# Retention scores: masked queries moved 512 columns wide over four row quarters, in place of masked keys loaded 128 wide over two

## The reference

```python
qh, kh, vh = (heads(q), heads(k), heads(v))          # [B, 16, T, 8]
gammas = decay_gammas(H)
dmask = jnp.where(causal[None], gammas[:, None, None] ** exponent[None], 0.0)
sim = jnp.einsum('bhnd,bhmd->bhnm', qh, kh) * scale
sim = sim * dmask[None]
yh = jnp.einsum('bhnm,bhmd->bhnd', sim, vh)
y = yh.transpose(0, 2, 1, 3).reshape(B, T, D)
y = y @ ow.T + ob
x = residual + y
```

## Time and profile before

| | before |
|---|---|
| median of 3 runs | 2216.85 us |
| lowest, highest | 2211.02, 2219.46 us |
| span of the profiled execution | 2256.3 us |
| TensorE busy | 1912.8 us (85%) |
| VectorE busy | 1357.7 us (60%) |
| ScalarE busy | 1044.8 us (46%) |
| GpSimd busy | 319.3 us (14%) |
| mean granted clock of TensorE | 0.821 of full |
| retention stage | about 900 to 1037 us of the span |

### The profile page before, as it was taken

How to read it: one execution, slowest core, us unless ns; L and a number is a source line. 1 busy time by engine, 2 the same in 40 slices (tenths; PEclk the granted TensorE clock), 3 DMA queues, 4 the chain that set the end, 5 groups by cost and what they waited for, 6 DMA issues and landing times.

```text
span 2256.3 us, 35340 instructions
## 1 busy us (share of the span) xinstructions
PE 1912.8 (85%) x12022; PEld 1293.6 (57%) x12022; DVE 1357.7 (60%) x4960; ACT 1044.8 (46%) x2490; POOL 319.3 (14%) x455
## 2 busy tenths in 40 slices
PE   6887777787778799999999888888899954999888
PEld 4464566666666566886555776555454542973333
DVE  3777888888888644676333485542121431569886
ACT  2433555665566423333444223454344313437667
POOL 0001000000000000330000002003126023406642
PEclk9999666667676568898999657998999967988989
DMA  2001100000000000000001100003013200635662
GB/s 111 1 13 36 32 22 22 19 19 25 19 19 19 34 1 1 2 3 2 0 1 75 40 1 1 1 15 97 13 12 50 89 14 30 113 69 91 98 103 40
DMA packets 93282, 76.09 MB, mean 34 GB/s; under 512 B 22320, under 2 KB 85168, under 8 KB 92336
## 3 DMA queue, kind: packets, MB, share of 16 engines
q1 hardware_dynamic: 85424, 65.31, 12.8%
q0 software_dynamic: 7680, 8.53, 2.0%
HBM read 48.86 MB, written 23.51 MB: 32 GB/s over the span
## 4 chain that ended last, share of the span: by engine, by line
PE 56%; DVE 23%; ACT 6%; DMA 4%; issue 4%; SPq 3%; another core or an unknown queue 1%; POOL 1%; DVEq 0%; PEld 0%; PEldq 0%; ACTq 0%; POOLq 0%
PE ps L204 52%; DVE sm L225 8%; ACT big L213 3%; DVE mw L225 3%; DMA d_pt<-big 3%; DVE big L217 2%; PE ps L208 2%; PE ps L2465 2%; SPq L2552 1%; DVE big L231 1%; DVE tmp L221 1%; ACT sm L213 1%; SPq L866 1%; DVE big L225 1%
## 5 line engine op out<-in xcount | busy, mean ns | idle before, releaser
L213 ACT ACTIVATE tmp<-ps,bi 128x512 f32<-128x512 f32 (+1 forms) x226 | 153.9, 684 | 200.8 <-PE ps L204 189.3
L204 PE MATMUL ps<-big,mw 128*128 128x512 f32 (+3 forms) x476 | 236.3, 593 | 11.6 <-DVEq L252 5.6
L213 ACT ACTIVATE sm<-sm 128x1 f32<-128x1 f32 x512 | 174.4, 341 | 106.6 <-DVE sm L225 96.0
L204 PE MATMUL ps<-ke,big 32*128 32x128 f32 (+2 forms) x1632 | 154.0, 296 | 62.3 <-ACT big L212 61.8
L204 PE MATMUL ps<-big,co 128*128 128x256 f32 (+1 forms) x360 | 180.5, 636 | 27.9 <-DMA bi<-bia 12.2
L213 ACT ACTIVATE big<-ps,co 128x512 f32<-128x512 f32 (+1 forms) x296 | 174.5, 648 | 61.3 <-PE ps L204 58.2
L204 PEld LDWEIGHTS ps<-ke,big 32*128 32x128 f32 (+2 forms) x1632 | 132.3, 195 | 87.4 <-ACT big L212 72.0
L231 DVE TENSOR_REDUCE big<-ps 128x2 f32<-128x512 f32 x256 | 161.2, 675 | 21.0 <-PE ps L204 20.7
L204 PE MATMUL ps<-ke 48*128 48x256 bf16 (+4 forms) x638 | 127.5, 315 | 34.7 <-DVE big L217 16.7
L204 PE MATMUL ps<-big,tmp 128*32 128x256 f32 (+2 forms) x1180 | 137.5, 424 | 22.9 <-DVE tmp L221 17.6
L217 POOL TENSOR_TENSOR big<-big,co 128x512 f32<-128x512 f32 x32 | 40.1, 1274 | 765.6 <-ACT big L212 765.6
(11 more groups left out here) (254 smaller groups left out, 3834.5 us busy)
## 6 DMA issues: line engine op xcount, KB each, us to landing
mw<-d_tab SPq DMA_DIRECT2D x32, 328.0 KB, 3.4
mw<-m SPq DMA_DIRECT2D x2, 4096.0 KB, 12.7
d_pt<-big SPq DMA_DIRECT2D x32, 192.0 KB
ke<-d_pt SPq DMA_DIRECT2D x72, 64.0 KB
big<-d_pt SPq DMA_DIRECT2D x72, 64.0 KB
mw<-d_pt SPq DMA_DIRECT2D x48, 64.0 KB
d_xs<-big SPq DMA_DIRECT2D x1, 2560.0 KB, 15.3
big<-d_xs SPq DMA_DIRECT2D x5, 512.0 KB, 6.4
```

The costliest lines, as they stand in the source:

```text
L204: return e.matmul(out, lhsT, rhs, start=start, stop=stop)
L213: return e.activation(out, in_, f, bias=K("zero")[0:out.shape[0], :] if bias is None else bias, scale=scale, **kw)
```

## The change

Three things change together.

The mask moves from the keys to the queries. ScalarE makes masked copies of the queries (`QM`, four instructions a block as before). The stationary operand is now a quarter of the plain keys (32 x 128), and the moving operand is the same quarter of all four masked queries, 32 x 512. One matmul gives the four heads of a quarter, and a half needs four matmuls, which are issued one after another as one burst and wait together.

The score banks rotate. A half takes two pairs of banks out of three pairs (banks 0 and 1, 2 and 3, 4 and 5), by the count `(2 * hh + p) % 3`. Its four matmuls wait for the first mask of the half before. Values, transposed keys and state move to bank 6, and the output of the block and its projection share bank 7. For that `ret_y_pe` now waits in first halves for the residual addition of the block before (`re_xa`) where it waited for a copy, and `ret_out_pe` and `ret_add_dve` move later: block n-2 is projected and added during block n, after the first scores of block n, and the addition stands ahead of the masks of block n on VectorE.

A mask covers two banks: four instructions of 128 x 1024 a block in place of eight of 128 x 512. On ScalarE the copy of the output (`ret_yc_act`) moves behind the copies of values and keys.

```diff
-        def ret_scores_pe(e, s):
-
-            n, h, p = s // 4, s // 2 % 2, s % 2
+        def pair(hh, p):
+            k = 2 * ((2 * hh + p) % 3)
+            return slice(k, k + 2)
+
+        def ret_scores_pe(e, hh):
+
+            n, h = hh // 2, hh % 2
             i, c0 = n % 2, n * S + 128 * h
-            if s % 4 == 0:
-                e.wait_ge(*re_km(4 * n + 4))
-            if s > 1:
-                e.wait_ge(*re_sm(2 * (s - 2) + 2))
-            for r in range(4):
-                for g in (2 * p, 2 * p + 1):
-                    q = mm(e, PS[:, g, 128 * r:128 * r + 128], KM[i][r32(g), r, 128 * h:128 * h + 128], QF[r32(g), c0:c0 + 128])
-                    if r == 3:
-                        q.then_inc(re_s.sem, 1)
+            if h == 0:
+                e.wait_ge(*re_qm(4 * n + 4))
+            if hh:
+                e.wait_ge(*re_sm(2 * hh - 1))
+            for g in range(4):
+                mm(e, PS[:, pair(hh, g // 2), :][:, g % 2, :], KF[r32(g), c0:c0 + 128], QM[i][r32(g), :, 128 * h:128 * h + 128]).then_inc(re_s.sem, 1)
...
             if h:
                 e.wait_ge(*re_sbd(n + 1))
-            elif n > 1:
-                e.wait_ge(*re_yc(n - 1))
-            e.wait_ge(*re_sm(4 * hh + 4))
+            elif n:
+                e.wait_ge(*re_xa(n))
+            e.wait_ge(*re_sm(2 * hh + 2))
...
-            for s in range(4 * NB + 2):
-                n, k = s // 4, s % 4
+            for hh in range(2 * NB + 2):
+                n, h = hh // 2, hh % 2
                 if n < NB:
-                    ret_scores_pe(e, s)
-                if s > 2 and k % 2:
-                    ret_y_pe(e, (s - 3) // 2)
-                if k == 1 and n + 1 < NB:
+                    ret_scores_pe(e, hh)
+                if h == 0 and n > 1:
+                    ret_out_pe(e, n - 2)
+                if h == 0 and n + 1 < NB:
                     ret_vk_pe(e, n + 1)
-                if k == 2 and 0 < n < NB:
-                    ret_out_pe(e, n - 1)
-                if k == 3 and n + 1 < NB:
+                if hh > 1:
+                    ret_y_pe(e, hh - 2)
+                if h == 1 and n + 1 < NB:
                     ret_kv_pe(e, n + 1)
...
-                act(e, KM[i][:, r, :], KF[:, c0:c0 + S], ACT.Identity, scale=K("rm", r, r + 1)).then_inc(re_km.sem, 1)
+                act(e, QM[i][:, r, :], QF[:, c0:c0 + S], ACT.Identity, scale=K("rm", r, r + 1)).then_inc(re_qm.sem, 1)
...
-            for s in range(4 * NB):
-                n, k, hh = s // 4, s % 4, s // 2
-                for g in (2 * (s % 2), 2 * (s % 2) + 1):
+            for hh in range(2 * NB):
+                n, h = hh // 2, hh % 2
+                if h == 0 and n > 1:
+                    ret_add_dve(e, n - 2)
+                for p in range(2):
                     if hh > 2:
                         e.wait_ge(*re_y(hh - 2))
-                    e.wait_ge(*re_s(2 * s + g % 2 + 1))
-                    tt(e, S1[hh % 3][:, g, :].rearrange("p (r n) -> p r n", r=4), PS[:, g, :].rearrange("p (r n) -> p r n", r=4),
-                       K("tri").rearrange("p (r n) -> p r n", r=1).broadcast_to((128, 4, 128)), MU).then_inc(re_sm.sem, 1)
-                if k == 3 and n:
-                    ret_add_dve(e, n - 1)
-                if k == 3 and n + 1 < NB:
+                    e.wait_ge(*re_s(4 * hh + 2 * p + 2))
+                    tt(e, S1[hh % 3][:, 2 * p:2 * p + 2, :].rearrange("p g (r n) -> p (g r) n", n=128),
+                       PS[:, pair(hh, p), :].rearrange("p g (r n) -> p (g r) n", n=128),
+                       K("tri").rearrange("p (r n) -> p r n", r=1).broadcast_to((128, 8, 128)), MU).then_inc(re_sm.sem, 1)
+                if h == 1 and n + 1 < NB:
                     ret_sbd_dve(e, n + 1)
```

## The result

The changed kernel takes 2176.07 us (median of four runs, 2175.51 to 2180.28) and the kernel before, measured beside it, 2216.22 us. The ratio is 0.9838 with a 95% interval of 0.9815 to 0.9861: 40 us faster, where 24.5 were forecast.

| comparison | before | changed | gain | ratio, 95% interval |
|---|---|---|---|---|
| first | 2216.22 | 2176.07 | 40.2 | 0.9838, 0.9815 to 0.9861 |
| second | 2215.17 | 2184.84 | 30.3 | 0.9860, 0.9835 to 0.9884 |
| third | 2257.86 | 2228.89 | 29.0 | 0.9868, 0.9828 to 0.9907 |
| fourth | 2217.82 | 2188.13 | 29.7 | 0.9865, 0.9849 to 0.9880 |

The account below looks back on a forecast made before the run. TensorE was taken to bound the stage: 1.67 us a block times 14.3 is 23.9, plus half of 1.5 at half clock, together 24.5, so 2216.85 - 24.5 = 2192.3 us. The range of 8 in 10 was 2182 to 2207.

Parts of the forecast that it names:

- What bounds it: In the stage's even part TensorE sets the pace, one block of 7.87 us after another, while other engines wait.
- Four abreast: TensorE's score burst: all four row quarters run side by side, 1.06 us a burst, saving 1.72 us a block.
- Rival A: Score bursts: four quarters of 512 columns go only two abreast, period 7.9 us, time 2217; chance 0.09 with partly abreast bursts.
- The mask: VectorE's mask of 128 x 1024: 1.22 us by itself, 1.14 behind another, bounds 1.07 and 1.37.
- Rival B: VectorE and its waits take over: mask 1.37 gives period 6.5 and 2197 us, mask 1.6 gives 2207; chance 0.09.
- The walk: One block followed through TensorE and VectorE: addition waits for projection, second burst for the first mask; period 6.2 us.
- The even blocks: Stage at full clock: 14.3 blocks, each going from 7.87 to 6.2 us, 23.9 us in all.
- The start of the stage: 17.7 us at half clock: a block goes from 12.11 to 10.3 us, worth 1.5 us, half taken by the tail.
- rival C: Clock stays at 1.2 GHz as TensorE stands still for VectorE; 2251 us with all 14.3 blocks low; chance 0.06.
- the prediction's own sign: Forecast is wrong if the stage is not 20 to 28 us shorter, or it is and the whole is not.

Follow-up runs that it names:

- wide start: Kernel before, with only the first two of its 16 blocks scored by masked queries moved 512 wide: 2210.2 us against 2217.8, ratio 0.9971.
- two orders: Changed kernel with projection issued ahead of the first burst, or the next block's state matmul moved ahead of the projection: ratios to the kernel before 0.9865 and 0.9889.
- wide scores alone: Kernel before with masked queries and 512-column score matmuls only; its two quarters a step, banks, order and masks kept: ratio 0.9936 to the kernel before.

## Why the prediction was wrong

**What bounds it, right.** TensorE set the pace and its pieces were the right unit of account: every piece that was to stay stayed within 0.1 us.

**Four abreast, right.** 1.07 a burst against 1.06. Rival A is out, as eight records of 512 columns take 1.14 together. An estimate from the 3.07 of the Trainium skill (TensorE: Matmul & The Clock Gate, Measured speedup vs the span model) gives 1.32 with the change of shape. The trace does not bear that out for a stream of bursts; the timeline's 1.07 decides.

**The mask, right.** 1.217 against 1.22, over two banks of PSUM. Rival B is out. The Trainium skill (TensorEngine Tiling (Array Packing), PSUM Bottleneck) says that the copy out of PSUM may become the bottleneck once TensorE is four times faster; the prediction put that as a certainty. The trace comes near it without reaching it: VectorE is busy for 53.00 of 61.96 us and the second burst waits for its first mask, but TensorE sets the period.

**The walk, right.** Period 6.2, addition late by 0.7, second burst held by the mask. It is right for a slightly other reason in the sum: projection and values next to each other take 1.29 instead of 1.38, and the wait for the mask takes that back.

**The even blocks, right.** Thirteen intervals of 7.87 became 6.20, 21.7 us, and the two last ones went from 9.88 to 9.27 together: 22.3 us against 23.9 forecast.

**The start of the stage, wrong. This is the step that failed.** The prediction said: "In the 17.7 us at half clock a block takes 12.11 before and an estimated 10.3 after", worth 1.5 us, half of it spent again. (Its terms, 23.9 and 0.75, add to 24.65 where it wrote 24.5.) It took the length of the low clock from the earlier trace rows as given and priced only the work inside it. From the stage's start to its first addition it is 24.2 us before and 17.1 after: 7.1 us, not 0.8. The clock stands at half for 6.4 to 6.5 us instead of 20 (once 13). The wide start in an otherwise unchanged kernel is enough for it, holding two quarters back in four bursts undoes it, and with 128 columns at a time it is the same (6.4), so it is shown that issuing four quarters abreast at the stage's start brings it. Why the clock answers to that is not shown. The prediction had this cause in its hands and gave it the wrong sign: rival C argued that waits keep the clock down, and in its answer stands that TensorE "does more in a unit of time than before", but no gain was drawn from that.

The stage then gives 7.1 + 22.3 = 29.4 us, the measured 136.8 to 107.4, and the three repeats of the comparison 29.0 to 30.3. By the prediction's own sign (a stage 20 to 28 us shorter) the stage alone makes it wrong.

**The remaining 10 us of the first comparison stay open.** The time fell below the range by them, and no step of the prediction accounts for them. Its interval (0.9815 to 0.9861) overlaps those of all three repeats. The trace of the changed kernel that goes with its runs has the same stage of 107.4 us, and outside the stage it takes 2066.2 us, against 2074.4 and 2085.7 in the second and the fourth comparison; so the changed kernel won them outside the stage, where no instruction differs. No trace of the kernel before goes with these runs. Traces of one chip (that of the second comparison) lie between 2065.2 and 2082.1 there, whatever the kernel, so spread of four runs a side is likely and not shown. Without it the forecast of 24.5 would have been 5 us short.

## What to carry to other kernels

Where TensorE's work is cut in row quarters, count how many are in flight in a slot, not how busy the engine is: four quarters issued together, one matmul each into a bank of its own, cost what two did (1.07 against 1.06 us here). Where a stage starts at the low clock, the length of that stretch belongs to the sum as a term of its own: here it was anything from 6.3 to 37.0 us, by how the first burst was issued. Look at the first bursts of the stage and what holds them apart. And walk every order once with all the semaphores: two orders that looked 0.1 and 0.2 us a block better on TensorE alone came out 0.14 and 0.22 worse, for a copy and for a cut that were just in time before.

## What the runs showed of the hardware

- The granted clock did not go by TensorE's busy share. It stayed at 0.50 through stretches in which TensorE was busy for 6.91 of 7.00 us with two quarters at a time, 30 us on end, and rose 6.8 us after it had fallen in all eleven traces whose first burst had four abreast, with TensorE busy for 5.86 of the 7.00 us around it. At the full level it stayed at 1.00 for 102 us of the kernel before, whose scores go two quarters at a time, and in the changed kernel through a wait of 1.01 us of TensorE (904.1 to 905.1).
- Four fp32 matmuls of 32 x 512 on four row quarters take 1.07 from their start to the next shape, two take 1.06 (wide scores alone).
- Of 128-column matmuls joined across two steps only a part overlaps (1.66 for both steps), of 512-column ones all (1.14).
- The kernel before takes 2215 to 2218 us on some chips and 2251 to 2258 on others. The stage of the changed kernel takes 107.4 us on all of them (four traces).
- With the same instructions, traces of one chip differ by 15 us outside the stage (2110.2 and 2125.6).
